# Turning the halves of a recurrent mixer kernel in another order

## The chip, the cores and the metric

The kernel runs on one core of a Trainium2 chip. The metric is the device time of one execution in microseconds (us), and a version's time is the median over its runs. A core has five engines that work side by side, each on its own queue of instructions: TensorE (PE) multiplies matrices, VectorE (DVE), ScalarE (ACT) and GpSimd (POOL) work element by element, and SyncE (SP) mostly issues DMAs. An engine takes its instructions strictly in order, and they wait for each other through semaphores, so an instruction that waits holds up all that is queued behind it.

## What is computed

The input is 4 sequences of 512 tokens with 1024 channels. Cut to what matters, the reference is

```python
xn = layernorm(x)
proj = xn @ in_proj_w.T                    # gate, hbc, dt
xBC = silu(causal_conv4(hbc))              # x, B, C per group
dt = softplus(dt + dt_bias);  dA = exp(-exp(A_log) * dt)
state_t = state_{t-1} * dA_t + (dt_t * x_t) B_t;  y_t = state_t C_t + D * x_t
s = (rms_of_group(y) * norm_weight * silu(gate)) @ out_proj_w.T
l = (xn / rms(xn)) @ [W_res, W_pre, W_post].T + base
g = silu(mix(sinkhorn(l_res), softmax(l_pre), softmax(l_post), xn))
out = x + s * g
```

The recurrence is worked out in its closed form over a sequence of 512: a matrix of decays between all pairs of tokens, multiplied by the products of C and B, is applied to dt * x. All is float32. TensorE multiplies a float32 matrix as three products of high and low parts (hi\*hi, hi\*lo, lo\*hi), so each operand that is streamed or held has to be split into both parts first.

## The kernel before

**Halves, groups, slots.** The 2048 tokens are worked in two halves of 1024 (two sequences, 8 token tiles of 128). For each half the kernel runs a front, then 8 groups of 8 heads. A group has 20 slots (SLOTS); in each, TensorE projects one tile of 128 channels for one sequence (`project`, L1101 to L1103, 24 matmuls) into one of two PSUM banks that alternate. Slots 0 to 11 carry channels that are convolved: ScalarE applies the last tap (`tap`, L616), VectorE the three others (`conv`, L839), ScalarE takes a tanh (L624), VectorE ends the silu (L851). Slots 12 to 19 are gate channels. ScalarE and VectorE also split the next weight tile into high (`split_hi`, L600) and low parts (`split_lo`, L821).

**Units.** A group's heads and sequences make 8 units, 0 to 7. For each one SP loads rows of cumulated decays (L363), ScalarE turns them into decays in two pieces (`exps`, L648 to L658, one for each of two heads), VectorE weighs them with C\*B (`weigh`, L877), TensorE transposes x (L1125), VectorE multiplies it by dt (L886), TensorE forms the products (`mult`, L1139), VectorE adds D\*x (`finish_y`, L899), ScalarE squares y (L671), and GpSimd adds up the squares (L476) and multiplies y with the gate (L467). Behind the last units come the channel sums on TensorE (L1149), a variance (L812), a root (L482), a trip through DRAM that spreads the root over the partitions (L372, L375), the scaling on GpSimd (L491) and the store (L378).

**Plans.** Which slot does which step of a unit is written out by hand in a `Plan`: FIRST for the first group of a half, LAST for the last, LATER for the others. `exp` lists the slot of each of the 16 pieces of decays, unit by unit. Slots from 20 on belong to the next group, and behind a half's last group they are worked by `drain`, which runs single slots of the old plan inside the next front, or behind the groups after the second half.

**The turn of the halves.** `front(1)` on each engine works the 8 token tiles of the second half, one t after the other, and drains slot 20 + t of the old group between. For a tile, VectorE takes statistics (`stats_of`, L933, L935), GpSimd makes the reciprocal root and the shift (`ln_rstd`, four instructions, L522 to L528), ScalarE scales the tile (`normalise`, L687), TensorE turns it in two half tiles n = 2t and 2t + 1 (`turn_stream`, L1171), ScalarE copies each half out of PSUM as the high part (`high`, L697), and VectorE takes the low part (`low`, L923). Tiles 0 to 3 have statistics and scale from before the turn, and half tiles 0 and 1 are turned in the last slot. There are three PSUM banks for the half tiles at this turn, so n = 3 waits for the low part of half tile 0. The lists STATS_AT, RSTD_AT and SCALE_AT say in which pass t of the front each tile is taken; their second entries are those of this turn.

Between them lie the small products (L1189 to L1191, 88 channels: dt and the logits), for two token tiles at a time, behind n = 5, n = 9 and at the end. They need the small weights in high (`small_hi`, ScalarE, L771) and low parts (`small_low`, GpSimd, L534). The pieces of the projection of slots 0 and 1 fill the rest of TensorE's front. Then it turns the small results back to tokens (L1219).

**Behind the front.** In slot 1 of the first group VectorE adds dt_bias to dt (z, L989), scales the logits (L993 to L997) and subtracts their maximum (L1004), all in `early`, ahead of that slot's convolution. At the top of slot 2 ScalarE takes the exponential of the logits (L706), works the softplus of z (L708 to L712, with a table load), and then splits the next weights and taps. TensorE's projection of slot 4 waits for the convolution of slot 2.

**Behind the second half** the product with out_proj_w runs in four passes, its operands loaded (L1337, L1338) and split (L1346, L1347, L1355, L1356) per 128 rows. The first pieces of it are woven into the last drained slots.

## Time and profile before

| what | value |
|---|---|
| median of 3 runs | 3055.89 us (3054.63 to 3057.09) |
| the profiled execution's own time | 3054.47 us |
| its span | 3053.0 us |
| busy time of TensorE | 3000.2 us |
| busy time of VectorE, ScalarE, GpSimd | 2128.1, 1763.6, 687.7 us |
| mean granted clock of TensorE | 0.997 |
| the front of half 0 | 0 to 45 us |
| the turn of the halves | 1160 to 1208 us |
| the last drained slots of half 1 | 2320 to 2340 us |

The span is what the trace covers; the execution's own time has 1.5 us more around it. Busy times of the engines overlap. A row of a time line has the start, the busy time, the engine, the line of the kernel, the operation, what it writes and reads, and how many such instructions the row merges; the bracket has the idle time of the engine ahead of it and who ended it. The granted clock is a share of full speed. Matmuls are pipelined, so their rows overlap a little.

### The profile page before, as it was taken

What the parts mean: (1) busy time and instruction counts of PE and PEld (TensorE: products, weight loads), DVE (VectorE), ACT (ScalarE), POOL (GpSimd) and SP (SyncE); (2) the same over time, 40 slices, a digit from 0 to 9 for tenths busy, and PEclk for the clock granted to TensorE, in tenths of its full rate; (3) what the DMA queues carried; (4) which work ended last, traced back from release to release, by engine and by line L of the source; (5) the groups of instructions that cost most, each with busy time, mean ns of one, the idle gap of its engine ahead of it and who ended that gap; (6) DMA issues with size and microseconds to landing.
All of it is one profiled execution on the core that took longest, in us unless ns stands there. A gap on an engine that the chain in (4) does not pass through costs nothing.

```text
span 3053.0 us, 45217 instructions
## 1 busy us (share of the span) xinstructions
PE 3000.2 (98%) x14352; PEld 2341.8 (77%) x14352; DVE 2128.1 (70%) x2648; ACT 1763.6 (58%) x3728; POOL 687.7 (23%) x575
## 2 busy tenths in 40 slices
PE   8999999999999998999999999999999999999998
PEld 7777777777777777777777777777777788887787
DVE  7667667576666685767666666766667878677877
ACT  5667575757666575576665757575665332234443
POOL 4222213121222134413222231212124000001112
PEclk9999999999999999999999999999999999999999
DMA  3534343443434353435243433434254444456665
GB/s 138 169 126 158 108 159 107 141 138 110 155 110 155 114 197 98 157 121 172 95 168 104 157 123 135 139 109 160 90 171 153 148 138 150 146 196 211 209 212 182
DMA packets 125532, 444.90 MB, mean 146 GB/s; under 512 B 17488, under 2 KB 21712, under 8 KB 109008
## 3 DMA queue, kind: packets, MB, share of 16 engines
q1 hardware_dynamic: 117552, 423.14, 41.1%
q0 software_dynamic: 4096, 14.68, 1.2%
q10 hardware_dynamic: 3744, 5.51, 0.6%
q8 instruction: 52, 0.85, 0.1%
q14 instruction: 88, 0.72, 0.1%
HBM read 397.86 MB, written 45.42 MB: 145 GB/s over the span
## 4 chain that ended last, share of the span: by engine, by line
PE 82%; issue 5%; DVE 4%; POOL 2%; ACT 2%; DMA 2%; DVEq 0%; SPq 0%; ACTq 0%; POOLq 0%
PE bank L1101 18%; PE bank L1103 17%; PE bank L1102 17%; PE bank L1139 9%; PE bank L1361 5%; PE bank L1362 5%; PE bank L1363 5%; PE bank L1113 2%; PE bank L1125 2%; DMA acc<-in_w_out 1%; PE bank L1149 1%; POOL gate L467 1%; DVE acc L839 1%; DVE x_lo L1356 1%; DVE x_lo L1355 1%
## 5 line engine op out<-in xcount | busy, mean ns | idle before, releaser
L1101 PE MATMUL bank<-x_hi,w_hi 128*128 128x512 f32 x2576 | 1024.6, 398 | 2.4 <-DVE acc L839 2.4
L1103 PE MATMUL bank<-x_hi,w_lo 128*128 128x512 f32 x2576 | 1003.0, 389 | 0.0
L1102 PE MATMUL bank<-x_lo,w_hi 128*128 128x512 f32 x2576 | 1000.9, 389 | 0.0
L839 DVE SCALAR_TENSOR_TENSOR acc<-bank,conv_w,acc 128x511 f32<-128x511 f32 (+2 forms) x576 | 430.8, 748 | 270.5 <-ACT acc L616 241.9
L1101 PEld LDWEIGHTS bank<-x_hi,w_hi 128*128 128x128 f32 x2576 | 484.1, 188 | 114.7 <-issue 22.2
L1103 PEld LDWEIGHTS bank<-x_hi,w_lo 128*128 128x128 f32 x2576 | 484.0, 188 | 102.6
L1102 PEld LDWEIGHTS bank<-x_lo,w_hi 128*128 128x128 f32 x2576 | 484.9, 188 | 93.6
L616 ACT ACTIVATE acc<-bank,tap_par 128x512 f32<-128x512 f32 x192 | 149.5, 779 | 517.0 <-PE bank L1103 486.0
L1361 PE MATMUL bank<-x_hi 128*128 128x512 f32 x1008 | 394.7, 392 | 8.9 <-DVE x_lo L1356 5.3
L1362 PE MATMUL bank<-x_lo,x_hi 128*128 128x512 f32 x1008 | 393.1, 390 | 0.0
L1363 PE MATMUL bank<-x_hi,x_lo 128*128 128x512 f32 x1008 | 392.9, 390 | 0.0
L877 DVE TENSOR_TENSOR units<-units,bc 128x2560 f32<-128x2560 f32 x128 | 370.4, 2893 | 5.2 <-ACT units L658 5.2
L1346 ACT ACTIVATE x_hi<-w_raw 128x1024 fp32r<-128x1024 f32 x126 | 133.6, 1060 | 390.4 <-PE bank L1363 279.8
L476 POOL TENSOR_TENSOR sums<-sums,sq 128x512 f32<-128x512 f32 x96 | 126.8, 1321 | 1010.2 <-ACT sq L671 1010.2
L652 ACT ACTIVATE units<-units,dec 128x384 f32<-128x384 f32 (+2 forms) x768 | 332.5, 499 | 0.0
L648 ACT ACTIVATE units<-units,cum 128x128 f32<-128x128 f32 x1024 | 325.0, 393 | 5.5 <-DMA units<-cum_scratch 5.5
L821 DVE TENSOR_TENSOR w_lo<-w_raw,w_hi 128x1024 fp32r<-128x1024 f32 x160 | 204.7, 1279 | 173.3 <-ACT w_hi L600 173.3
L858 DVE SCALAR_TENSOR_TENSOR gate<-th,gate 128x512 f32<-128x512 f32 x128 | 128.0, 1000 | 269.0 <-ACT gate L636 269.0
L1139 PE MATMUL bank<-units,dtx 128*64 128x512 f32 (+3 forms) x2048 | 304.9, 440 | 0.8 <-DVE units L877 0.8
L467 POOL TENSOR_TENSOR gate<-gate,units 128x512 f32<-128x512 f32 x128 | 190.8, 1495 | 345.8 <-DVE gate L858 275.8
L1139 PEld LDWEIGHTS bank<-units,dtx 128*64 128x64 f32 x2048 | 135.6, 137 | 165.4 <-issue 145.4
L1355 DVE TENSOR_TENSOR x_lo<-w_raw,x_hi 128x1024 fp32r<-128x1024 f32 x126 | 168.1, 1334 | 134.2 <-ACT x_hi L1347 133.7
(165 smaller groups left out, 3408.0 us busy)
## 6 DMA issues: line engine op xcount, KB each, us to landing
units<-cum_scratch SPq DMA_DIRECT2D x128, 1280.0 KB, 6.7
w_raw<-in_w_in SPq DMA_DIRECT2D x160, 512.0 KB, 3.7
w_raw<-y_scratch SPq DMA_DIRECT2D x128, 512.0 KB, 3.6
y_scratch<-gate SPq DMA_DIRECT2D x32, 1024.0 KB, 6.5
acc<-in_w_out SPq DMA_DIRECT2D x128, 256.0 KB, 3.8
xbc<-in_x SPq DMA_DIRECT2D x16, 512.0 KB, 5.6
units<-in_x SPq DMA_DIRECT2D x16, 512.0 KB, 3.7
rstd_b<-rc_scratch SPq DMA_DIRECT2D x32, 256.0 KB, 4.3
```

Of the source, the lines that this page charges most:

```text
L467: pool.tensor_tensor(part, part, y[:, u % 2, :], ALU.mult).then_inc(gated, 1)
L648: op = act.activation(part, part, ACT.Relu, bias=mix.cum[:, CHUNKS * q + k, head], scale=-1.0)
L652: act.activation(part, part, ACT.Exp, bias=mix.dec[:, CHUNKS * q + k, head])
L839: dve.scalar_tensor_tensor(acc[:, s % 2, back:], bank_proj[s % 2][:, 0:SEQ - back], mix.conv_w[:, at, m, 3 - back:4 - back], acc[:, s % 2, ...
L877: dve.tensor_tensor(attn[u % RING][:, :, :], attn[u % RING][:, :, :], bc[:, q, :].unsqueeze(1).to_broadcast([P, 2, SPAN]), ALU.mult).then_ ...
L1101: pe.matmul(out, w_hi[m % 2][:, k, :], hi, start=(k == 0), stop=False)
L1102: pe.matmul(out, w_hi[m % 2][:, k, :], lo, start=False, stop=False)
L1103: mm = pe.matmul(out, w_lo[m % 2][:, k, :], hi, start=False, stop=(k == KT - 1))
L1139: mm = pe.matmul(bank_y[u % 2][h * HD:(h + 1) * HD, k * P:SEQ], dtx[:, u % 2, k, h * HD:(h + 1) * HD], attn[u % RING][:, h, OFFSET[k]:OFFS ...
L1361: pe.matmul(self.bank[t][:, :], self.y_hi[n][j][:, toks], self.w_hi[n][j], start=first, stop=False)
L1362: pe.matmul(self.bank[t][:, :], self.y_hi[n][j][:, toks], self.w_lo[n][j], start=False, stop=False)
L1363: return pe.matmul(self.bank[t][:, :], self.y_lo[n][j][:, toks], self.w_hi[n][j], start=False, stop=last)
```

## The change

Six edits. (1) In the plan LAST the decays of units 5 and 7 take a slot together each (15 and 18) and those of unit 6 slots 16 and 17; the last piece was in slot 19 before. (2) At the turn VectorE takes the statistics of tile 4 in pass 1 instead of pass 0. (3) GpSimd takes the roots of tiles 5 and 6 both in pass 2, ahead of the drained slot 22 (whose last step is a multiply with the gate), and that of tile 7 in pass 5; the low part of the small weights moves from pass 1 to pass 2, behind these roots. (4) ScalarE makes the high part of the small weights in pass 1 instead of pass 0. (5) TensorE does the drained slot 21, the products of unit 7, ahead of transpose n = 3 instead of behind it. (6) VectorE's logits in slot 1 of both halves' first group come behind that slot's convolution; z stays ahead of it.

```diff
 LAST = Plan(cb=[5, 7], load=[4, 5, 7, 10, 12, 14, 15, 17], mult=[9, 11, 13, 14, 16, 18, 20, 21],
-            gate_from=CONV_SLOTS, exp=[6, 7, 8, 9, 10, 11, 11, 12, 13, 14, 15, 16, 17, 18, 18, 19])
+            gate_from=CONV_SLOTS, exp=[6, 7, 8, 9, 10, 11, 11, 12, 13, 14, 15, 15, 16, 17, 18, 18])
...
-STATS_AT = [{t: [0, 1, 2] if t == 0 else [t + 2] for t in range(NT - 2)}, {0: [4], 2: [5], 3: [6], 5: [7]}]
+STATS_AT = [{t: [0, 1, 2] if t == 0 else [t + 2] for t in range(NT - 2)}, {1: [4], 2: [5], 3: [6], 5: [7]}]
...
-RSTD_AT = [{t: [t] for t in range(NT)}, {1: [4], 3: [5], 4: [6], 6: [7]}]
+RSTD_AT = [{t: [t] for t in range(NT)}, {1: [4], 2: [5, 6], 5: [7]}]
...
                 for i in RSTD_AT[half].get(t, []):
                     ln_rstd(half, i)
-                if t == (1 if half else 2):
+                if t == 2:
                     small_low(half)
...
             for t in range(NT):
-                if t == 0 and half:
+                if t == 1 and half:
                     act.wait_ge(proj_done, SLOTS * half * GROUPS)
                     act.wait_ge(e.small_loaded, 16)
                     act.activation(small_hi, small_raw, ACT.Copy).then_inc(e.small_step, 1)
...
-        def early(half, s):
+        def early(half, s, late=False):
...
-            if s == 1:
+            if s == 1 and not late:
...
                     dve.tensor_tensor(z[:, tiles, :], part[:, :, 0:HEADS], over_tiles(dt_bias, HEADS),
                                       ALU.add).then_inc(e.dt_step, 1)
+            if s == 1 and late:
+                for i, b in enumerate(bank_small):
+                    part = b[:, 0:4 * SMALL].rearrange("p (t c) -> p t c", c=SMALL)
+                    tiles = slice(4 * i, 4 * i + 4)
                     if i == 0:
+                        dve.wait_ge(e.to_tokens, 2)
                         dve.wait_ge(e.rms_step, 4)
                     dve.tensor_tensor(logits[:, tiles, :], part[:, :, HEADS:],
...
                     if s or plan is not FIRST:
                         conv(g, at, s)
+                    if plan is FIRST and s == 1:
+                        early(half, s, late=True)
                     if s:
                         silu(g, s - 1)
...
                 if half and n == 2:
                     drain(piece, half - 1, SLOTS, SLOTS + 1)
                     pe.wait_ge(dtx_done, UNITS * g)
+                if half and n == 3:
+                    drain(piece, half - 1, SLOTS + 1, SLOTS + 2)
                 turn_stream(half, n)
-                if half and h:
+                if half and h and t > 1:
                     drain(piece, half - 1, SLOTS + t, SLOTS + t + 1)
```

## Rows read from the trace of the kernel before

**Rows 1.** The page's busy times of the engines over the span.

```profile
PE 3000.2 (98%) x14352; PEld 2341.8 (77%) x14352; DVE 2128.1 (70%) x2648; ACT 1763.6 (58%) x3728; POOL 687.7 (23%) x575
```

**Rows 2.** Waits of TensorE over the run: total, times, longest, in us.

```profile
PE bank L1171 <- DVE x_lo L923: 10.1, 3, 5.1
...
PE bank L1101 <- DVE acc L839: 2.4, 2, 1.4
```

**Rows 3.** Engines' busy time by stretches of the turn; PEclk behind POOL's.

```profile
core 0: us, PE busy (x) PEld busy (x) DVE busy (x) ACT busy (x) POOL busy (x), PEclk, DMA share, GB/s
1160.00:1170.00 10.00, 4.89 (x26) 2.37 (x24) 6.91 (x9) 7.57 (x16) 6.12 (x7) 0.83 0.12 22
1170.00:1180.00 10.00, 7.65 (x69) 6.92 (x65) 5.93 (x12) 2.73 (x4) 6.62 (x7) 1.00 0.24 83
1180.00:1190.00 10.00, 7.37 (x45) 6.79 (x45) 4.51 (x9) 5.02 (x7) 7.85 (x18) 0.83 0.28 55
```

**Rows 4.** TensorE's time line at the turn, where it waited.

```profile
1166.73 1.09 PE L1171 MATMUL bank<-ident,xbc 128*128 128x128 f32 x4 [5.11 <-DVE x_lo L923]
...
1174.09 0.63 PE L1171 MATMUL bank<-ident,xbc 128*128 128x128 f32 x4 [2.35 <-DVE x_lo L923]
...
1183.24 0.85 PE L1171 MATMUL bank<-ident,xbc 128*128 128x128 f32 x4 [2.63 <-DVE x_lo L923]
```

**Rows 5.** VectorE's time line at the start of the turn.

```profile
1160.74 1.28 DVE L933 BATCH_NORM_STATS2 rows<-xbc 128x6 f32<-128x512 f32 x2
...
1162.50 2.83 DVE L877 TENSOR_TENSOR units<-units,bc 128x2560 f32<-128x2560 f32 x1 [0.24 <-ACT units L658]
...
1165.90 1.28 DVE L923 TENSOR_TENSOR x_lo<-bank,x_hi 128x512 fp32r<-128x512 f32 x2
```

**Rows 6.** ScalarE's time line at the turn, its longest wait for GpSimd.

```profile
1180.65 1.24 ACT L687 ACTIVATE xbc<-xbc,ln_shift,rstd 128x1024 f32<-128x1024 f32 x1 [4.20 <-POOL ln_shift L528]
```

**Rows 7.** GpSimd's time line at the turn.

```profile
1169.17 1.69 POOL L534 TENSOR_TENSOR w_lo<-units,w_hi 128x704 fp32r<-128x704 f32 x1
...
1176.53 1.30 POOL L476 TENSOR_TENSOR sums<-sums,sq 128x512 f32<-128x512 f32 x1 [3.22 <-ACT sq L671]
...
1179.16 0.21 POOL L522 TENSOR_SCALAR lv<-mv 128x1 f32<-128x1 f32 x1
...
1180.38 0.24 POOL L528 TENSOR_SCALAR ln_shift<-ln_shift 128x1 f32<-128x1 f32 x1
```

**Rows 8.** DMA issues from 1160 to 1180 us: KB each, median us to landing.

```profile
xbc<-in_x SPq DMA_DIRECT2D x2, 512.0 KB, 3.5
```

**Rows 9.** VectorE's time line in slot 1 of half 1.

```profile
1208.26 0.42 DVE L989 TENSOR_TENSOR units<-bank,rows 128x256 f32<-128x256 f32 x1 [0.49 <-PE bank L1219]
...
1210.23 0.23 DVE L1004 TENSOR_TENSOR rstd_b<-rstd_b 128x64 f32<-128x64 f32 x1
1210.37 2.31 DVE L839 SCALAR_TENSOR_TENSOR acc<-bank,conv_w,acc 128x511 f32<-128x511 f32 x3
```

**Rows 10.** ScalarE's time line in slot 2 of half 1.

```profile
1210.49 0.26 ACT L706 ACTIVATE rstd_b<-rstd_b 128x64 f32<-128x64 f32 x1 [1.34 <-DVE rstd_b L1004]
...
1213.78 1.04 ACT L600 ACTIVATE w_hi<-w_raw 128x1024 fp32r<-128x1024 f32 x1
```

**Rows 11.** TensorE's time line at the start of slot 4, both halves.

```profile
57.83 0.47 PE L1101 MATMUL bank<-x_hi,w_hi 128*128 128x512 f32 x1 [1.41 <-DVE acc L839]
...
1220.40 0.47 PE L1101 MATMUL bank<-x_hi,w_hi 128*128 128x512 f32 x1 [1.00 <-DVE acc L839]
```

**Rows 12.** TensorE's time line behind half 1, where it waited.

```profile
2331.02 0.50 PE L1361 MATMUL bank<-x_hi,w_hi 128*128 128x512 f32 x1 [1.52 <-DVE x_lo L1356]
...
2340.39 0.61 PE L1361 MATMUL bank<-x_hi,w_hi 128*128 128x512 f32 x1 [1.20 <-DVE var_eps L812]
...
2369.09 0.50 PE L1361 MATMUL bank<-x_hi 128*128 128x512 f32 x1 [2.49 <-DVE x_lo L1356]
```

**Rows 13.** VectorE's time line behind half 1.

```profile
2324.24 2.83 DVE L877 TENSOR_TENSOR units<-units,bc 128x2560 f32<-128x2560 f32 x1 [1.69 <-ACT units L658]
...
2340.18 0.15 DVE L812 TENSOR_SCALAR var_eps<-bank 128x4 f32<-128x4 f32 x1
```

## The prediction

> **What bounds the kernel now.** I read four views: the page's busy times, the waits of TensorE, the granted clock by stretches, and then the time line of each engine around the places where TensorE waits. TensorE is busy for 98% of the span [rows 1]. So only its idle time, some 50 us in all, and the time it runs at the lower clock can be won, and any other engine matters only where TensorE waits for it. Two of the waits lie where the diff works. At the turn of the halves TensorE waits 10.1 us in three pieces for VectorE's x_lo (L923), and at the fifth projection slot of a half's first group it waits for a convolution (L839), 2.4 us over both halves [rows 2]. The three pieces at the turn are 5.11, 2.35 and 2.63 us [rows 4]. The granted clock is 0.83 over 1160 to 1170 and again over 1180 to 1190, and 1.00 between [rows 3]: part of each stretch ran at the lower of the two levels (1.2 instead of 2.4 GHz), which loses 10 x 0.17 = 1.7 us of work. So the turn holds 10.1 + 3.4 = 13.5 us that a better order could win. The pieces have different causes. In the first, TensorE needs x_lo of half tile 0 (1165.90), behind the weighting of the last unit (1162.50) and the statistics of tile 4 (1160.74) [rows 5]. The second has the late products behind the first transpose as its cause. In the third, ScalarE waits 4.20 us at 1180.65 for the shift of tile 5 [rows 6], because GpSimd takes its root (1179.16) only behind the addition of the last unit (1176.53) and its gate multiply [rows 7].
>
> **The change, part by part.**
>
> *1. The turn.* Times are those of the profiled execution. Up to 1160.75 us nothing that TensorE waits for moves: the decays are six pieces in five slots either way, ScalarE has room for them (3.1 us each). The decays of unit 7 are done by 1156.7 instead of 1162.5, so VectorE weighs it at 1160.75 to 1163.6 (2.83 us [rows 5]), finishes y of unit 6 by 1164.2, takes the statistics of tile 4 to 1165.65, and x_lo of half tile 0 to 1166.3. That is the same moment as before: the statistics have only changed places with the weighting. But TensorE now does the products of unit 7 meanwhile, 1163.7 to 1166.1 (sixteen matmuls, 2.4 us at the full clock), and has the transposes n = 3 and 4 behind it by 1167.7, where before it began n = 4 at 1171.1. y of unit 7 comes 3.7 us sooner. x_lo of half tile 2 follows the statistics of tile 5 (1.5 us) and is there at 1169.5. So n = 5 runs to 1170.3, the channel sums to 1171.1. Here 4.3 us are won.
>
> The small products are next, and they need the low part of the small weights (L534), which GpSimd before made at 1169.17, in 1.69 us, long ahead of its use [rows 7]. The change puts it behind the roots of tiles 5 and 6. GpSimd: the square of unit 6 is ready at 1168.7, addition and gate to 1171.3 (1.3 us each), two roots of four instructions, 1.46 us each by the one that begins at 1179.16, to 1174.2, then the low part to 1175.9. The statistics of tile 6 don't add to this: its load is issued when transpose n = 3 is done, 1167.1, and lands 3.5 us later [rows 8], so they are ready by 1172.1. **TensorE waits from 1171.1 to 1176.1**, a new wait of 5 us, and starts the small products 0.6 us later than before. It is as long as the 5.11 us one, so I charge one drop of the clock, 1.7 us. From there everything is ready: ScalarE has tiles 5 and 6 scaled, the wait of 2.63 us and its drop are gone. Before, 12.7 us lay between the start of the first small products and the end of the second; now 12.7 - 2.6 - 1.7 + 1.7 = 10.1. The turn ends at 1186.2 to 1186.6 instead of 1188.2: **a gain of 1.6 us**, 3.7 at best (no drop, 2 us less wait), nothing at worst (a landing of 5 us instead of 3.5, or slowed GpSimd work). The result's scaling on GpSimd ends 1.7 us earlier and is still well ahead of VectorE's z. SP's two last tile loads go out 0.8 and 4 us earlier, which nobody waits for.
>
> *2. The logits behind a convolution.* VectorE adds dt_bias at 1208.26, ends the logits at 1210.46 and then convolves, three instructions, 2.31 us from 1210.37 [rows 9]. Who waits for the logits is ScalarE: its exponential starts at 1210.49, and its queue holds the rest of softplus, with a table load, and then the high part of the next weights at 1213.78 [rows 10]. VectorE idles until it has them, and through its queue this delays the third convolution, for which TensorE waits 1.00 us at 1220.40, and 1.41 us at the same place of half 0 [rows 11]. So the chain from the logits to that wait has no slack at all. The convolution that goes ahead moves the exponential by the distance from its start to that of the next instruction, 2.23 us; all behind it follows. What moves forward, that convolution, was no one's wait: TensorE ran two slots without a gap. Cost: 2.23 us in this half. In half 0, where the rows repeat, ScalarE's tap is a little late: 2.1. **Sum 4.3 us.** The waits are then 3.2 and 3.5 us.
>
> The trace has no such wait in dense work, so the clock after it must be bounded. Waits of 1.00, 1.41, 2.35 and 2.49 us left the clock at 1.00; those of 2.63 (in sparse work) and 5.11 us did not. The bounds are nothing and 1.7 us each; the new waits lie above 2.63, so I take the drop: 3.4 us. The Trainium skill, "TensorE: Matmul & The Clock Gate", section "Why this matters for your kernels", says the same against this change: idle gaps of TensorE between bursts of matmuls are to be kept short, since its clock else goes back to half. By it the sum would have both drops; without it the sum is 3.4 us lower.
>
> *3. The end of half 1.* LAST's decays serve it too. VectorE's last weighting (2324.24) waits 1.69 us for ScalarE there, TensorE 1.52 us at 2331.02 for the split behind it, and 1.20 us at 2340.39 for a variance (written at 2340.18) [rows 12, 13]. With unit 7's decays done by 2320.1, the weighting starts 1.8 us earlier. That also lets ScalarE square unit 5 3 us earlier, so GpSimd's additions come sooner and hold up VectorE less. TensorE's products of unit 7 no longer wait 0.8 us, the split is ready 2.5 to 3 us earlier, and the last variance follows by 2.2 to 3. But a wait comes after: 2.49 us at 2369.09 [rows 12], at the end of a chain (variance, root, two small transfers, GpSimd's scaling, store, load, split) which moves only with that variance. What TensorE gains beyond it is waited out there. **Gain 2.5 us**; bounds nothing (the scaling is slowed more) and 3.4.
>
> *The sum*: 4.3 + 3.4 - 1.6 - 2.5 = +3.6 us. On the profiled 3054.47 us that is 3058.1. That execution lies 1.4 us under the median of the runs, 3055.89, so the median to expect is **3059.4 us**. A measurement of this kernel can tell about 0.2%, 6.1 us, from no change: my sum is inside.
>
> **The rivals.**
>
> *The clock keeps up* (no drop after the 3.3 us waits, none or one at the turn). For it: 2.49 us in dense work cost no clock. The sum is then 4.3 - 2.5 - 1.6 to 3.7 = +0.2 to -1.9, some 3055. Chance 0.25, no change that can be told.
>
> *Faster: the turn's reordering works as a whole.* If GpSimd had the low part of the small weights by 1171, the turn would lose its second and third pieces, half of the first and both drops: about 9 of the 13.5 us. With 2.5 at the end and 4.3 for the logits it gives 3055.9 - 7.2 = 3048.7. It decides if small_low waits for no more than one root. Against it: the loop takes both roots of its pass first, and TensorE can't pass the small products. Chance 0.07.
>
> *Slower: the delayed logits cost more than their convolution.* The place is ScalarE's queue at the fifth slot. VectorE has almost no idle time over the next 30 us, so 2.2 us that it loses need not be made up, and each later product of the stream mixer hangs on it. If 1.5 us more of waits follow in each half, the price is 4.3 + 3.4 + 3 = 10.7, and less 4.1 for turn and end it is +6.6: 3062.5. It decides from 6.1 - 3.6 = 2.5 us beyond my price. For it: VectorE's queue; against it: everything behind the third convolution shifts together with TensorE. Chance 0.15.
>
> *The change does nothing*: all of it is made up behind the turn. TensorE has no waits to make up with for a thousand us, so this could hold only for part 3. Chance 0.03 (3056).
>
> **The numbers.** The forecast has 0.50. Its own range is 3056 to 3062. The four rivals take the other 0.50. For 8 in 10 the range must take in the clock rival and half of each outer one: 3051.0 to 3063.0. Faster by over 0.2% (under 3049.8): 0.07. Slower (over 3062.0): 0.15. Within: 0.78.
>
> **What would show it.** In the changed profile: TensorE idle some 2 us, 2 us and then about 5 us before the first small product (L1189), released by GpSimd's w_lo; no wait near 1183; the small products over by 1186.5. At the fifth slot of both halves, waits for L839 of 3.2 to 3.5 us, with a clock under 1.00 just after. At the end no wait for L877, a variance about 2.5 us earlier and a wait for x_lo near 2369 that has grown. I am wrong if the first small product starts before 1174, if the two waits for L839 stay under 2 us, or if the end of half 1 moves by other than the sum of the first two parts, some +6 us, ahead of part 3.

## The result, and the profile after the change

The changed kernel takes 3062.78 us in the median of 22 runs (3059.68 to 3068.0). The kernel before, in 22 runs beside it, takes 3056.4 us (3054.1 to 3060.64). The ratio is 1.0021, with a 95% interval of 1.0014 to 1.0027: 6.4 us slower. That it is slower is clear; that it is slower by over 0.2%, the bound that was named, is not, since the interval begins at 0.14%. The forecast was +3.6 us, 3059.4 us in all, and the range went to 3063.0. So sign and main term were right, some 3 us were missed, and the range held by only 0.2 us, which is partly luck.

The profiled execution took 3061.02 us, with a span of 3059.5 us and a mean granted clock of 0.995 (3053.0 us and 0.997 before). Lines are shifted: the projection L1101 to L1103 is L1108 to L1110 now, L1139 is L1146, L1149 is L1156, L1171 is L1178, L1189 is L1196, L1219 is L1228, L1004 is L1009, and L1355, L1356, L1361 are L1364, L1365, L1370. This is the page's line of busy times, against [rows 1]:

```profile
PE 3004.6 (98%) x14352; PEld 2343.4 (77%) x14352; DVE 2125.8 (69%) x2648; ACT 1763.5 (58%) x3728; POOL 691.7 (23%) x575
```

The totals hardly move. The waits of TensorE at the turn (1155 to 1190 us) and the one for the convolution over the whole run say more; the columns are total, times and longest, in us. Against [rows 2]:

```profile
PE bank L1196 <- POOL w_lo L534: 4.2, 1, 4.2
PE bank L1146 <- DVE units L877: 3.0, 1, 3.0
PE bank L1178 <- DVE x_lo L923: 1.5, 1, 1.5
PE bank L1156 <- POOL sums L476: 0.5, 1, 0.5
...
PE bank L1108 <- DVE acc L839: 6.4, 2, 3.2
```

At the turn 10.1 us of one kind became 9.2 us of four kinds, with one new name at the top: the low part of the small weights. The wait for the convolution went from 2.4 to 6.4 us.

**Where the time went.** A kernel whose TensorE is busy for 98% is best compared by milestones on TensorE's own time line. Five of them cut the span into stretches: the small results turned back in half 0 (L1219 of before), the first transposes of the turn, the small results turned back in half 1, the first product of the output projection (L1361), and the matmul behind the last chain wait, at 2369.09 in [rows 12]. For each stretch the length is the difference of two starts.

| stretch | before | after | difference | forecast |
|---|---|---|---|---|
| start to L1219 | 44.69 | 45.13 | +0.4 | 0 |
| rest of half 0 | 1107.02 | 1111.17 | +4.2 | +3.8 |
| the turn | 55.94 | 56.54 | +0.6 | -1.6 |
| rest of half 1 | 1114.96 | 1118.83 | +3.9 | +3.9 |
| end of half 1, to the last chain wait | 46.48 | 44.94 | -1.5 | -2.5 |
| output passes | 683.9 | 682.9 | -1.0 | 0 |

The differences add up to 6.5 us, as the spans do. The first and the last row are not touched by the change: over the experiments below, which don't touch them either, the start took from 45.0 to 47.3 us and the output passes from 681.3 to 690.2 us. So 1 us there in any one profile means nothing, and the stretches between are to be read, not the spans.

**The logits.** This is TensorE's time line at the fifth slot of both halves, in the changed kernel, against [rows 11]:

```profile
60.08 0.47 PE L1108 MATMUL bank<-x_hi,w_hi 128*128 128x512 f32 x1 [3.21 <-DVE acc L839]
...
1227.81 0.47 PE L1108 MATMUL bank<-x_hi,w_hi 128*128 128x512 f32 x1 [3.24 <-DVE acc L839]
```

The stretches behind them, and those of the turn, against [rows 3]; PEclk, the granted clock, stands behind POOL's busy time:

```profile
core 0: us, PE busy (x) PEld busy (x) DVE busy (x) ACT busy (x) POOL busy (x), PEclk, DMA share, GB/s
60.00:70.00 10.00, 9.92 (x35) 7.43 (x35) 9.86 (x10) 4.02 (x7) 6.34 (x5) 0.83 0.32 106
1160.00:1170.00 10.00, 7.01 (x41) 4.36 (x41) 8.11 (x6) 5.53 (x11) 4.82 (x2) 1.00 0.38 141
1170.00:1180.00 10.00, 6.62 (x34) 4.48 (x30) 8.23 (x17) 4.92 (x7) 5.45 (x13) 0.68 0.30 105
1180.00:1190.00 10.00, 7.12 (x45) 7.10 (x46) 1.11 (x4) 2.46 (x4) 6.04 (x7) 0.64 0.01 0
...
1220.00:1230.00 10.00, 6.76 (x27) 5.25 (x26) 7.57 (x12) 5.39 (x7) 4.24 (x3) 0.91 0.00 0
1230.00:1240.00 10.00, 10.00 (x39) 7.50 (x39) 9.82 (x12) 4.09 (x8) 5.52 (x4) 0.92 0.50 163
```

The waits were forecast at 3.5 and 3.2 us and are 3.21 and 3.24. Behind each, part of the work ran at the lower of the two levels: 0.17 of 10 us at 60, and 0.09 and 0.08 of 10 us from 1220 to 1240. That is 1.7 us both times.

Half 0 has one small cost more, which was not forecast. These are TensorE's waits at the products of C and B (L1113, L1120 now) from 40 to 1140 us, before and after; half 1's are alike, 1.9 us in both:

```profile
PE bank L1113 <- DVE bc L868: 1.9, 5, 0.4
...
PE bank L1120 <- DVE bc L868: 2.7, 5, 0.7
```

They are 0.8 us longer. With 1.8 us more of wait at the fifth slot (3.21 less 1.41) and 1.7 us of clock this makes 4.3 us, where the stretch shows 4.2.

The delay's way through ScalarE's queue can be read off its time line in slot 2 of half 1, against [rows 10]:

```profile
1217.89 0.26 ACT L706 ACTIVATE rstd_b<-rstd_b 128x64 f32<-128x64 f32 x1 [3.56 <-DVE rstd_b L1009]
...
1221.18 1.05 ACT L600 ACTIVATE w_hi<-w_raw 128x1024 fp32r<-128x1024 f32 x1
```

ScalarE now idles 3.56 us (1.34 before) and then, behind softplus, makes the high part of the weights. From the milestone L1219 to that instruction were 1213.78 - 1207.65 = 6.13 us; now they are 1221.18 - 1212.84 = 8.34, so 2.21 us more, where 2.23 was the price.

**The turn.** Here the forecast failed. TensorE's time line, where it waited, against [rows 4]:

```profile
1169.19 3.61 PE L1146 MATMUL bank<-units,dtx 128*64 128x512 f32 x16 [2.99 <-DVE units L877]
1172.73 1.49 PE L1178 MATMUL bank<-ident,xbc 128*128 128x128 f32 x8
1175.73 0.63 PE L1178 MATMUL bank<-ident,xbc 128*128 128x128 f32 x4 [1.51 <-DVE x_lo L923]
1176.87 1.77 PE L1156 MATMUL bank<-mask,sums 128*128 128x1 f32 x8 [0.51 <-POOL sums L476]
1182.88 0.48 PE L1196 MATMUL bank<-x_hi,w_hi 128*88 128x256 f32 x1 [4.24 <-POOL w_lo L534]
```

The pieces are 2.99, 1.51, 0.51 and 4.24 us where about 2, 2 and 5 were forecast. The sixteen products of unit 7 took 3.61 us, where 2.4 were charged: the clock had dropped already there, one wait earlier than in the forecast. The cause of the first wait is seen on VectorE and GpSimd. VectorE's time line, against [rows 5]:

```profile
1165.33 3.81 DVE L877 TENSOR_TENSOR units<-units,bc 128x2560 f32<-128x2560 f32 x1
...
1169.72 1.27 DVE L933 BATCH_NORM_STATS2 rows<-xbc 128x6 f32<-128x512 f32 x2
```

and GpSimd's, against [rows 7]:

```profile
1165.18 1.27 POOL L476 TENSOR_TENSOR sums<-sums,sq 128x512 f32<-128x512 f32 x1 [6.34 <-ACT sq L671]
1166.41 3.86 POOL L467 TENSOR_TENSOR gate<-gate,units 128x512 f32<-128x512 f32 x1
...
1175.54 1.28 POOL L476 TENSOR_TENSOR sums<-sums,sq 128x512 f32<-128x512 f32 x1 [2.75 <-ACT sq L671]
1176.77 1.27 POOL L467 TENSOR_TENSOR gate<-gate,units 128x512 f32<-128x512 f32 x1
1178.12 0.22 POOL L522 TENSOR_SCALAR lv<-mv 128x1 f32<-128x1 f32 x1
...
1179.66 0.21 POOL L522 TENSOR_SCALAR lv<-mv 128x1 f32<-128x1 f32 x1
...
1181.07 1.67 POOL L534 TENSOR_TENSOR w_lo<-units,w_hi 128x704 fp32r<-128x704 f32 x1
```

The same weighing took 2.83 us in [rows 5] and takes 3.81 here. GpSimd's addition began 0.15 us ahead of it and has its normal 1.27 us; the gate multiply behind it shows 3.86 us for what takes 1.27 elsewhere, and ends within 1.2 us of the weighing's end. A reader can take this as turns at one resource: addition (to 1166.45), weighing (2.8 us, to 1169.14), gate multiply (1.2 us, to 1170.27). So not every microsecond of these durations is work. Experiment 9 tests this reading. Then the rest is as foreseen: two roots 1.54 us apart, and the low part behind both.

**The end of half 1.** Three rows of TensorE's time line, against [rows 12]:

```profile
2338.32 0.50 PE L1370 MATMUL bank<-x_hi,w_hi 128*128 128x512 f32 x1 [0.65 <-DVE x_lo L1365]
...
2347.69 0.75 PE L1370 MATMUL bank<-x_hi,w_hi 128*128 128x512 f32 x1 [1.21 <-DVE var_eps L812]
...
2376.61 0.50 PE L1370 MATMUL bank<-x_hi 128*128 128x512 f32 x1 [2.47 <-DVE x_lo L1365]
```

What lies ahead of this stretch is 9.06 us later than before (2331.67 against 2322.61). Less that, the three starts are 1.8, 1.8 and 1.5 us earlier than in [rows 12]. VectorE's time line, against [rows 13], shows why it is no more:

```profile
2331.53 2.81 DVE L877 TENSOR_TENSOR units<-units,bc 128x2560 f32<-128x2560 f32 x1
...
2334.92 1.66 DVE L1364 TENSOR_TENSOR w_lo<-w_raw,w_hi 128x1024 fp32r<-128x1024 f32 x1
2336.51 1.76 DVE L1365 TENSOR_TENSOR x_lo<-acc,x_hi 128x512 fp32r<-128x512 f32 x1
```

The weighing waits for nothing any more and starts 1.8 us earlier by the same count. But the splits behind it still take 1.66 and 1.76 us; where GpSimd is idle, they take 1.21 and 0.68 in this same trace (2324.68 and 2325.81). The forecast had GpSimd's additions out of VectorE's way, and they are not: the first one showed 2.62 us from 2332.88, held up behind the weighing.

### The profile page after: what moved, and what is told of

It reads as the page before. It is cut to its first block, busy times and chain, and to the rows that moved or that the text cites. A ratio compares the mean times of both kernels' runs of the same rounds, so it can differ in the third digit from the quotient of the medians.

```text
span 3059.5 us, 45219 instructions
## 1 busy us (share of the span) xinstructions
PE 3004.6 (98%) x14352; PEld 2343.4 (77%) x14352; DVE 2125.8 (69%) x2648; ACT 1763.5 (58%) x3728; POOL 691.7 (23%) x575
## 4 chain that ended last, share of the span: by engine, by line
PE 45%; issue 5%; DVE 4%; DMA 2%; ACT 2%; POOL 1%; DVEq 0%; SPq 0%; ACTq 0%; POOLq 0%
PE bank L1108 9%; PE bank L1110 9%; PE bank L1109 8%; PE bank L1146 4%; PE bank L1370 4%; PE bank L1372 4%; PE bank L1371 4%; DMA acc<-in_w_out 1%; PE bank L1120 1%; DVE x_lo L1365 1%; PE bank L1132 1%; DVE x_lo L1364 1%; DVE bc L1668 1%; DMA th<-in_x 1%; ACT x_hi L1356 1%
## 5 line engine op out<-in xcount | busy, mean ns | idle before, releaser
L1108 PE MATMUL bank<-x_hi,w_hi 128*128 128x512 f32 x2576 | 1024.6, 398 | 6.4 <-DVE acc L839 6.4
L1110 PE MATMUL bank<-x_hi,w_lo 128*128 128x512 f32 x2576 | 1003.0, 389 | 0.0
L839 DVE SCALAR_TENSOR_TENSOR acc<-bank,conv_w,acc 128x511 f32<-128x511 f32 (+2 forms) x576 | 430.9, 748 | 275.7 <-ACT acc L616 246.7
L1108 PEld LDWEIGHTS bank<-x_hi,w_hi 128*128 128x128 f32 x2576 | 484.4, 188 | 119.5 <-issue 26.3
L1110 PEld LDWEIGHTS bank<-x_hi,w_lo 128*128 128x128 f32 x2576 | 484.3, 188 | 103.3
L1370 PE MATMUL bank<-x_hi 128*128 128x512 f32 x1008 | 394.2, 391 | 8.2 <-DVE x_lo L1365 4.8
L1355 ACT ACTIVATE x_hi<-w_raw 128x1024 fp32r<-128x1024 f32 x126 | 133.5, 1060 | 390.7 <-PE bank L1372 252.3
L1146 PE MATMUL bank<-units,dtx 128*64 128x512 f32 (+3 forms) x2048 | 305.1, 440 | 3.0 <-DVE units L877 3.0
L1146 PEld LDWEIGHTS bank<-units,dtx 128*64 128x64 f32 x2048 | 135.6, 137 | 167.4 <-issue 145.5
L1364 DVE TENSOR_TENSOR x_lo<-w_raw,x_hi 128x1024 fp32r<-128x1024 f32 x126 | 168.6, 1338 | 134.1 <-ACT x_hi L1356 133.4
```

Source lines behind the costliest of these rows:

```text
L839: dve.scalar_tensor_tensor(acc[:, s % 2, back:], bank_proj[s % 2][:, 0:SEQ - back], mix.conv_w[:, at, m, 3 - back:4 - back], acc[:, s % 2, ...
L1108: pe.matmul(out, w_hi[m % 2][:, k, :], hi, start=(k == 0), stop=False)
L1110: mm = pe.matmul(out, w_lo[m % 2][:, k, :], hi, start=False, stop=(k == KT - 1))
L1146: mm = pe.matmul(bank_y[u % 2][h * HD:(h + 1) * HD, k * P:SEQ], dtx[:, u % 2, k, h * HD:(h + 1) * HD], attn[u % RING][:, h, OFFSET[k]:OFFS ...
L1370: pe.matmul(self.bank[t][:, :], self.y_hi[n][j][:, toks], self.w_hi[n][j], start=first, stop=False)
```

## The experiments

I had four theories to test, each against a rival: the loss comes from the logits, through ScalarE's queue; the turn's gain is eaten by the low part's place; the slow weighing is GpSimd's doing; and part of the loss is the clock. All kernels were measured beside the kernel before. "Turn" is the length of that stretch, as in the table above (55.94 us before). 0.2% is 6 us, so a median of about ten runs tells some 3 us, and below that the stretches of the profile decide.

**1. The logits alone.** The kernel before, and of the change only this:

```diff
-        def early(half, s):
+        def early(half, s, late=False):
...
-            if s == 1:
+            if s == 1 and not late:
...
+            if s == 1 and late:
...
                     if s or plan is not FIRST:
                         conv(g, at, s)
+                    if plan is FIRST and s == 1:
+                        early(half, s, late=True)
```

> The kernel before with the logits behind the convolution and nothing else. Theory A (the convolution that now goes ahead delays ScalarE's exponential, the next weights and TensorE's fifth slot by its own length, and the longer wait costs the clock): two waits for L839 of 3.2 us instead of 1.00 and 1.41 us, a granted clock of 0.83 in the 10 us behind each, together 4.0 + 3.4 = 7.4 us slower than before. Rival (most of the change's loss comes from the turn of the halves, and the delayed logits are made up by slack on VectorE): waits as in the kernel before and less than 3 us slower.

Measured: 3063.49 us against 3056.99, ratio 1.0021 (1.0012 to 1.0030), +6.5 us. TensorE's time line at the fifth slots:

```profile
60.30 0.47 PE L1108 MATMUL bank<-x_hi,w_hi 128*128 128x512 f32 x1 [3.20 <-DVE acc L839]
...
1225.49 0.47 PE L1108 MATMUL bank<-x_hi,w_hi 128*128 128x512 f32 x1 [3.23 <-DVE acc L839]
```

and the stretches behind them:

```profile
60.00:70.00 10.00, 9.70 (x40) 7.44 (x41) 9.86 (x11) 3.82 (x6) 6.55 (x5) 1.00 0.30 106
1220.00:1230.00 10.00, 6.76 (x23) 5.06 (x23) 9.76 (x16) 3.80 (x5) 4.23 (x3) 0.83 0.13 32
```

The loss of the whole change is in this part. The waits are the same to 0.01 us as in the changed kernel, but the clock is not: it dropped in half 1 and stayed at 1.00 in half 0. The rest of half 0 was 2.4 us longer than before and that of half 1 3.8 us. The waits account for 1.8 + 0.8 us in half 0 (the same 2.7 instead of 1.9 us for the products of C and B) and for 2.2 us in half 1, so the drop in half 1 cost some 1.6 us. A drop behind a 3.2 us wait is thus a matter of the execution, not a certainty; I had it as a choice between bounds, and both bounds occur.

**2. Everything but the logits.** The changed kernel with that part taken back.

```diff
-                    if plan is FIRST and s == 1:
-                        early(half, s, late=True)
```

> The changed kernel with the logits put back ahead of the convolution. Theory A: the loss of 4.1 us in the first half and 3.9 us behind the turn is gone, the turn costs 0.6 us and the end of the second half gives 2.5 us back, so about 2 us faster than before. Rival (the turn itself is what costs): no faster than before.

Measured: 3055.30 us, 0.9993 (0.9984 to 1.0002), -1.7 us; the interval takes in no change. The turn is 55.7 us, with waits of 2.99 for the weighing, 1.91 for x_lo, and then this one in TensorE's time line:

```profile
1178.90 0.48 PE L1189 MATMUL bank<-x_hi,w_hi 128*88 128x256 f32 x1 [4.96 <-POOL w_lo L534]
```

So turn and end together gain 0.2 + 1.5 us, not the 4.1 forecast. The rows give the 4.96 us to the low part, whose place the next but one tests. (Experiments 1 and 2 add up to +4.8 us, and the whole change is +6.4; each has 3 us of width, so this says nothing.)

**3. The decays alone.**

```diff
-            gate_from=CONV_SLOTS, exp=[6, 7, 8, 9, 10, 11, 11, 12, 13, 14, 15, 16, 17, 18, 18, 19])
+            gate_from=CONV_SLOTS, exp=[6, 7, 8, 9, 10, 11, 11, 12, 13, 14, 15, 15, 16, 17, 18, 18])
```

> The kernel before with only the new slots of the last group's decays. Theory A (unit 7's decays were late only behind the second half, since at the turn the statistics of tile 4 filled VectorE's time): the turn keeps its waits of 5.1, 2.4 and 2.6 us within 0.5 us, and the end of the second half is 2.5 us shorter, with the wait for L877 gone; 2.5 us faster in all. Rival (the earlier decays are worth more at the turn as well, as VectorE can weigh sooner): 4 us or more faster.

Measured: 3055.76 us, 0.9998 (0.9989 to 1.0007). The time can't tell it from no change; the stretches can. The end of half 1 is 44.76 us instead of 46.48, and VectorE no longer waits for the decays there: the whole gain of part 3 is this one edit, and it is 1.7 us (1.5 in the changed kernel), not 2.5. The turn gains nothing by it (waits of 5.57, 2.35 and 2.62 us against [rows 4]), since the statistics still stand ahead of the weighing. The first wait is even 0.46 us longer: with the decays done earlier ScalarE squares unit 5 earlier, and GpSimd's addition and multiply begin at 1160.94 and 1162.18, 3.0 and 4.6 us earlier against the turn's first transposes. Both are ahead of the weighing (1162.52), and it takes 3.60 us here.

**4. The low part back in its old place.** Experiment 2, and:

```diff
-                if t == 2:
+                if t == (1 if half else 2):
                     small_low(half)
```

> The changed kernel without the logits' edit, and with the low part of the small weights back in pass 1, behind the root of tile 4, as before. Theory A (this one step on GpSimd, queued behind two roots, is what takes back the turn's gain): TensorE's wait of 4.2 us for w_lo is gone, the small products start some 4.5 us earlier than in the changed kernel, and the whole is 4 to 6 us faster than all but the logits, that is 6 to 8 us faster than before. Rival (the turn is held by VectorE, whose weighing of unit 7 took 3.8 us instead of 2.8 beside GpSimd's gate multiply, and by the clock): the time freed comes back as a wait for x_lo at the next transposes, and it is less than 2 us faster than all but the logits.

Measured: 3050.80 us, 0.9976 (0.9966 to 0.9985), -6.2 us. The waits of TensorE at the turn:

```profile
PE bank L1139 <- DVE units L877: 3.0, 1, 3.0
PE bank L1171 <- DVE x_lo L923: 2.4, 2, 2.0
```

The wait for the low part is gone, and the turn is 51.2 us. One line of the change, a place in GpSimd's queue, costs 4.5 us at the turn, and 4.5 us between the medians of experiments 2 and 4. Up to 1.8 us of it can be the clock: by the granted clock from 1160 to 1190 us experiment 2 loses 5.2 us, experiment 4 3.4. With the line undone, the other edits of the turn gain 4.7 us. But the wait for the weighing is still 2.99 us.

**5. The gate multiply held back.** Experiment 4, and GpSimd's gate multiply of unit 5 waits until VectorE has weighed unit 7, so that it can't collide with it.

```diff
+            if hold:
+                pool.wait_ge(attn_done, UNITS * g + UNITS)
...
-                gate_y(g, u)
+                gate_y(g, u, hold=plan is LAST and half == 0 and u == 5)
```

> The kernel with the low part early, and GpSimd's gate multiply of unit 5 at the turn held until VectorE has weighed unit 7. Theory B (the weighing took 3.8 instead of 2.8 us because GpSimd's gate multiply ran beside it): the weighing is back at 2.8 us, the gate multiply at 1.3 instead of 3.9 us, TensorE's wait for L877 is 2.0 instead of 3.0 us; 1 us faster than with the low part early. Rival (the weighing is slow for another reason, such as x loads that land then): the weighing stays above 3.5 us and nothing is won.

Measured: 3051.56 us, 0.9982 (0.9973 to 0.9991), the turn 52.6 us. VectorE's time line:

```profile
1160.85 3.82 DVE L879 TENSOR_TENSOR units<-units,bc 128x2560 f32<-128x2560 f32 x1
```

and GpSimd's:

```profile
1160.70 1.28 POOL L478 TENSOR_TENSOR sums<-sums,sq 128x512 f32<-128x512 f32 x1 [6.33 <-ACT sq L673]
1164.83 1.28 POOL L469 TENSOR_TENSOR gate<-gate,units 128x512 f32<-128x512 f32 x1 [2.85 <-DVE units L879]
```

The turn is 1.4 us longer than in experiment 4, and that is the clock: from 1160 to 1190 us it loses 5.1 us here and 3.4 there. The products of unit 7 took 3.88 us here and 2.38 there, behind the same wait of 2.99 us; there the clock fell one wait later, behind 2.02 us at 1170.93 (0.66 over 1170 to 1180). The multiply is out of the way and has its normal 1.28 us, but the weighing is as slow as it was. My theory that the multiply slows it fell. What remains is the addition that begins 0.15 us ahead of it; experiment 9 holds that one.

**6. ScalarE's split ahead of softplus.** Experiment 1 with its delayed logits, but in slot 2 ScalarE does the next weights' high part and the tap first, and the exponential and softplus behind them:

```diff
-                if plan is FIRST:
+                if plan is FIRST and s != 2:
                     early(half, s)
...
+                    if plan is FIRST and s == 2:
+                        early(half, s)
```

> The kernel with only the logits behind the convolution, and ScalarE's queue in slot 2 turned: the high part of the next weights and the tap go ahead of the exponential and the softplus. Theory A (the delay reached TensorE through this queue alone): no wait for L839 at the fifth slot of either half though the logits still come late, and 2 to 3 us faster than the kernel before, 9 us faster than the logits alone. Rival (VectorE's own queue carries the delay as well: the logits' 1.4 us and the softmax stand ahead of the third convolution there): a wait of 1 to 2 us stays.

Measured: 3052.93 us, 0.9992 (0.9983 to 1.0001), -2.6 us, where experiment 1 was at +6.5. The waits of TensorE from 40 to 1300 us:

```profile
PE bank L1180 <- DVE x_lo L925: 7.5, 2, 5.1
PE bank L1122 <- DVE bc L870: 2.7, 5, 0.7
PE bank L1249 <- ACT units L740: 1.1, 2, 0.6
```

No wait for L839 is left, in either half, though the logits are as late as before. So the delay reaches the fifth slot through one place, the split and the tap behind softplus in ScalarE's queue; and [rows 10, 11] already held 2.4 us to be had there. It isn't all of the harm: the 2.7 us for the products of C and B stay (1.9 before, and in experiment 8, which has the logits in their old place), so 0.8 us in half 0 come another way. Which way is not shown.

**7. Statistics a tile later.** Experiment 4 with the statistics, scalings and roots of the turn spread so that x_lo of half tile 2 goes ahead of the statistics of tile 5:

```diff
-STATS_AT = [..., {1: [4], 2: [5], 3: [6], 5: [7]}]
-SCALE_AT = [..., {2: [4], 3: [5], 4: [6], 6: [7]}]
-RSTD_AT = [..., {1: [4], 2: [5, 6], 5: [7]}]
+STATS_AT = [..., {1: [4], 3: [5], 4: [6], 5: [7]}]
+SCALE_AT = [..., {2: [4], 4: [5], 5: [6], 6: [7]}]
+RSTD_AT = [..., {1: [4], 3: [5], 4: [6], 5: [7]}]
```

> The kernel with the low part early, and the statistics, roots and scales of tiles 5 and 6 one pass later, so that x_lo of half tiles 2 and 3 comes ahead of the statistics of tile 5. Theory (the remaining wait of 2.0 us for x_lo is this order of VectorE's): it falls to about 0.5 us, the turn is 1.5 us shorter, and up to 1.7 us more where the clock no longer falls; 1.5 to 3 us faster than with the low part early. Rival (what is freed comes back where ScalarE scales tile 5 ahead of a copy, as before the change): no faster.

Measured: 3050.75 us, 0.9983 (0.9974 to 0.9992), the turn 51.1 us as in experiment 4. The wait for x_lo shrank from 2.02 to 0.53 us, and this came in its place:

```profile
1174.65 1.05 PE L1149 MATMUL bank<-mask,sums 128*128 128x1 f32 x8 [1.51 <-POOL sums L476]
```

The channel sums need GpSimd's addition, which comes behind the same late products: where one wait was removed, the next shows, and none of my expectations had that. The clock doesn't hide a gain: the two profiles had it low at other moments (the products of unit 7 took 3.98 us here and 2.38 in experiment 4), but by the windows from 1160 to 1190 us both lose alike, 3.5 and 3.4 us. So one wait took the other's place, and no gain is shown. The 1.4 us against experiment 5 are its clock, which loses 5.1 us.

**8. Together.** The held multiply, the later statistics and the early split of ScalarE, with the logits in their old place.

> All that helped together: the changed kernel without the logits' edit, the low part early, the gate multiply held, the statistics of tiles 5 and 6 a pass later, and ScalarE's split and tap ahead of the exponential. If the gains add: 6 us of the low part early, 1 of the gate, 1.5 to 3 of the statistics, 2.4 of the splits: 11 to 12 us faster than the kernel before, about 3045 us. If they share one cause (the clock): 8 us.

Measured: 3045.62 us, 0.9970 (0.9959 to 0.9980), -10 us. By the stretches: half 0 -1.9, turn -6.4, half 1 -1.4, end -1.6. The waits at the turn are those of experiment 7, and the 1.6 us that the turn is shorter (49.5 against 51.1 us) are the clock's: it loses 1.7 us here and 3.5 there.

**9. The addition held instead.** Experiment 8, but the wait stands ahead of GpSimd's addition of unit 5 and not ahead of the multiply:

```diff
-        def add_square(g, u):
+        def add_square(g, u, hold=False):
...
+            if hold:
+                pool.wait_ge(attn_done, UNITS * g + UNITS)
```

> All that helped together, and now GpSimd's addition of unit 5 (not only its gate multiply) held until VectorE has weighed unit 7. Theory C (the one of the two engines that starts second waits for the whole instruction of the other; the weighing lost 1.0 us because the addition had begun 0.15 us ahead of it): the weighing is back at 2.8 us and TensorE's wait for it at 2.0 us instead of 3.0; 1 us faster than with only the gate held (3045.6 us), and up to 1.7 more if the clock then keeps up. Rival (something other than GpSimd slows this weighing): it stays at 3.8 us.

Measured: 3046.31 us, 0.9969 (0.9957 to 0.9982). VectorE's time line:

```profile
1159.14 2.82 DVE L881 TENSOR_TENSOR units<-units,bc 128x2560 f32<-128x2560 f32 x1
```

and TensorE's:

```profile
1162.01 2.37 PE L1143 MATMUL bank<-units,dtx 128*64 128x512 f32 x16 [1.99 <-DVE units L881]
...
1169.07 1.05 PE L1153 MATMUL bank<-mask,sums 128*128 128x1 f32 x8 [1.83 <-POOL sums L478]
```

The weighing is back at 2.82 us, TensorE waits 1.99 us for it (which is the "about 2" of the forecast), and the products run at the full clock in 2.37 us. That settles the cause. The time is the same as in experiment 8, though the small products start 1.7 us earlier (19.9 against 21.6 us behind the turn's first transposes). The addition that was held is late for the channel sums, 1.83 against 1.51 us, and above all the clock, which in experiment 8 was low over the products of unit 7, is low over the small products here, from 1170.3 on: one drop in each, 1.7 us, and it only changed its place.

**10. The low part behind one root.** Experiment 2, with the low part between the roots of tiles 5 and 6:

```diff
+                    if half and i == 5:
+                        small_low(half)
-                if t == 2:
+                if t == 2 and not half:
                     small_low(half)
```

> The changed kernel without the logits' edit, and with the low part of the small weights between the roots of tiles 5 and 6 instead of behind both. Theory A (each root ahead of it delays TensorE by its own length): the wait for w_lo, 5.0 us with both ahead, falls to 3.5 us, and 1.5 us are won. Rival (the wait is a matter of tile 6's load, which comes late): it falls by less than 0.7 us or by more than 2.5 us.

Measured: 3054.08 us, 0.9995 (0.9986 to 1.0004), the turn 55.6 us. The profiled execution was the slowest of the eleven, 3059.07 us. TensorE's time line:

```profile
1177.34 0.49 PE L1191 MATMUL bank<-x_hi,w_hi 128*88 128x256 f32 x1 [2.63 <-POOL w_lo L534]
```

The wait shrank from 4.96 to 2.63 us, by 2.3 us, more than the 1.5 of the theory and less than the 2.5 of its rival. The small products start 25.1 us behind the turn's first transposes, where experiment 2 has 26.3 (experiment 4: 21.3). In this profile nothing of it reaches the end of the turn (55.6 against 55.7 us), but the clock explains that: from 1160 to 1190 us it loses 6.9 us here and 5.2 in experiment 2. So a root ahead may well cost about its own length; this pair of profiles can't show it. My "faster" rival said that one root ahead would be enough for it to hold. It is not: the larger part of the delay stands ahead of both roots: GpSimd waits 2.76 us for the square of unit 6, and its addition and multiply take another 2.5 us. Only ahead of those is the low part in time.

**11. The wait filled.** The changed kernel, with twelve more matmuls ahead of the fifth slot's projection, into a bank that is free there; nobody reads their result.

```diff
+                if plan is FIRST and s == 4:
+                    for n in range(12):
+                        pe.matmul(core.bank[7][:, :], mix.x_hi[:, 0, 0:P], mix.x_hi[:, 0, 0:SEQ], start=True, stop=True)
```

> The changed kernel, whole, with twelve more matmuls (128 by 512, operands that lie ready, into a free bank, result unused) on TensorE ahead of slot 4's projection in each half's first group; they fill 2.7 of the 3.2 us that it waits for L839 there. Theory D (behind such a wait the clock falls and costs 1.7 us on top): the granted clock is 1.00 in the 10 us behind both places, the wait left is 0.5 us, and the kernel is 2 to 3.5 us faster than the changed one (3062.8 us) although it does more work. Rival (the clock has nothing to do with the difference): the same time as the changed kernel.

Measured: 3059.07 us, 1.0012 (1.0003 to 1.0021), +2.8 us against the kernel before, where the changed kernel without them is at +6.4. The stretches behind the waits:

```profile
60.00:70.00 10.00, 9.50 (x40) 6.90 (x39) 9.79 (x12) 2.63 (x4) 7.22 (x5) 1.00 0.30 105
1220.00:1230.00 10.00, 9.47 (x42) 7.56 (x41) 7.26 (x12) 5.40 (x7) 4.03 (x3) 1.00 0.00 0
```

Of the two waits 0.50 and 0.53 us are left, and the clock stays at 1.00. The projection starts no earlier, since its convolution is as late as before, and still half 0 is 1.6 us shorter than in the changed kernel and half 1 1.8 us. So each drop cost about the 1.7 us that the windows say. The Trainium skill, "TensorE: Matmul & The Clock Gate", section "Why this matters for your kernels", wants the idle gaps between bursts of matmuls kept short; this run agrees, 3.7 us faster with the gaps filled. It isn't so every time: in half 0 of experiment 1 the clock stayed at 1.00 behind 3.20 us.

**12. The turn's first wait filled.** Experiment 9, with two float32 matmuls ahead of the products of unit 7; nobody reads their result.

```diff
+                    for _ in range(2):
+                        pe.matmul(core.bank[7][:, :], core.ident[:, :], core.mask[:, :], start=True, stop=True)
```

> The kernel with the addition held, and two more matmuls (128 by 512 float32, about 1 us each, result unused) on TensorE ahead of unit 7's products at the turn, where it waits for the weighing. Theory D: the granted clock stays at 1.00 over the turn, 1.7 us faster than with the addition held if that one still lost its clock there, otherwise the same. Rival: the fillers run beyond the wait and it is up to 1 us slower.

Measured: 3045.66 us, 0.9969 (0.9958 to 0.9981), the turn 49.5 against 49.4 us. The granted clock is 0.83 over 1170 to 1180 in both. Nothing was won, nor lost. At the wait that was filled there was nothing to win, since the clock had stayed up behind it in experiment 9 (products in 2.37 us); the drop that is left comes behind the other short waits, which weren't filled. What would remove it stays open.

Experiments 8, 9 and 12 can't be told apart. Each is some 10 us (0.3%) faster than the kernel before and 17 us faster than the changed one.

**The turn with and without its clock.** Loss is 10 us times what the granted clock lacks to 1, added over the three windows from 1160 to 1190 us.

| | turn | loss | difference |
|---|---|---|---|
| experiment 4 | 51.2 | 3.4 | 47.8 |
| experiment 5 | 52.6 | 5.1 | 47.5 |
| experiment 7 | 51.1 | 3.5 | 47.6 |
| experiment 8 | 49.5 | 1.7 | 47.8 |
| experiment 9 | 49.4 | 1.7 | 47.7 |
| experiment 12 | 49.5 | 1.7 | 47.8 |

Without the clock the six are alike to 0.3 us. (The loss is an upper bound of what the clock cost, since a low clock during a wait costs nothing.) What is shown at the turn is the gain of the low part's old place with the new order (experiment 4). Holding the multiply or the addition, and the later statistics, moved waits about and shortened nothing beyond the clock, whose state in one profile each may be chance.

## Why the prediction was right or wrong

*Part 2, the logits: right, but for a small term.* "The waits are then 3.2 and 3.5 us" against 3.24 and 3.21, 2.21 us of delay at the split against 2.23, and 3.8 and 3.9 us forecast against 4.2 and 3.9 found. Experiment 1 puts the whole loss there and experiment 6 shows the way that most of it takes. The small term is the 0.8 us of waits for the products of C and B in half 0, put at nothing. "I take the drop: 3.4 us" held in the profiled execution. As a rule it is too sure: one of four such waits (two in the changed kernel, two in experiment 1) left the clock at 1.00. And the list of waits behind which the clock stayed up was not complete: in the same trace it was 0.83 over 2340 to 2350, behind waits of 1.52 and 1.20 us [rows 12].

*Part 1, the turn: the step that failed* is "so VectorE weighs it at 1160.75 to 1163.6 (2.83 us)". It starts when I said (1165.33 less the 4.59 us by which the turn began later is 1160.74), but takes 3.81 us. I had taken the duration from a row in which VectorE had begun first. The evidence lay in the trace of before, in this row of GpSimd's time line, which I did not use:

```profile
1163.55 2.90 POOL L476 TENSOR_TENSOR sums<-sums,sq 128x512 f32<-128x512 f32 x1 [9.29 <-ACT sq L671]
```

It ran beside the weighing of 1162.50 and shows 2.90 us where its like take 1.3: there GpSimd was the one that waited. The change moved the weighing 1.75 us earlier, and the addition 3.0 us (1163.55 before, 1165.18 less 4.59 = 1160.59 now), to just ahead of it, and so turned round who waits. The earlier addition is edit (1)'s doing, as experiment 3 shows. The prediction used it for the end of half 1 ("lets ScalarE square unit 5 3 us earlier") and not at the turn, where it let nothing move up to 1160.75 and read the new decays as "six pieces in five slots either way"; in the new plan they are in four. Of "the same moment as before" 1.0 us is lost, and behind a wait of 2.99 instead of 2 us the clock dropped already for the products of unit 7: 3.61 instead of 2.4 us (in experiment 9 the wait is 1.99 us, and they take 2.37). These two terms, 1.0 + 1.2 = 2.2 us, are the size of the miss. They pass on through the transposes behind the products and ScalarE's copy of them, behind which the square of unit 6 queues. That square, the addition behind it, the two roots and the low part follow as forecast, each 2.2 us late: w_lo is ready at 1182.74, against 1175.9 + 4.6 = 1180.5. From the first small product to the end of the turn the forecast gained 2.6 us, and 2.3 came.

*"Charge one drop of the clock" in the turn: wrong in number.* The windows from 1170 to 1190 are at 0.68 and 0.64, which loses 6.8 us where 1.7 were charged and the kernel before loses 3.4. Some of it costs nothing: the clock was low through the 4.24 us of the wait for w_lo, and the channel sums ahead of that wait (1.77 us at 1176.87) only shortened it. What counts is the products of unit 7, and the first twenty of the small ones at 0.21 us apiece, up to 1187.

*The cause of the new wait: right.* "The change puts it behind the roots of tiles 5 and 6", and experiment 4 gives 4.5 us back for that one line (up to 1.8 us of them the clock's).

*Part 3, the end of half 1: right in kind, too large.* "The weighting starts 1.8 us earlier" is met. The failed term is "GpSimd's additions come sooner and hold up VectorE less": the splits still take 1.66 and 1.76 us. So all that follows moves by 1.8 us and not by 2.5 to 3. The 2.49 us wait at the end of the chain did not grow (2.47): TensorE's work ahead of it and the chain moved together.

*The rivals.* "The clock keeps up" did not hold in the profiled execution, and did in half 0 of experiment 1. "Faster: the turn works as a whole" had its mechanism right in experiment 4, -6.2 us without the logits' part, but its point of decision wrong (experiment 10). "The delayed logits cost more than their convolution" gave nearly the time that was found, 3062.5, and mostly by the wrong cause: of its 1.5 us more of waits in each half, 0.8 came in half 0 and none in half 1, which came out at +3.9. A median that fits a rival is no evidence for it; the stretches are.

The sum over the parts: 3.6 forecast, 2.2 at the turn, 1.0 at the end of half 1, 0.35 in half 0, 0.4 ahead of it, and -1.0 in passes that the change doesn't touch, gives 6.5.

Two slips in the sums change nothing: 3055.89 + 3.6 is 3059.5, not 3059.4, and the turn's "3.7 at best" is the gain with no drop alone; with "2 us less wait" as well it would be over 5.

## What to carry to other kernels

Before you move a small instruction of an in-order engine behind others, count its whole queue up to the new place, and place it by the consumer that has the least slack, not by its cost. When you move an instruction of VectorE with two operands in SBUF, look at what GpSimd starts around the new moment, and at what the same change does to that: who starts first keeps its normal duration, and the other shows the wait as duration. Compare kernels that a busy TensorE bounds by milestones on its time line, and set the granted clock of each stretch beside its length before you call a difference a gain. Read a clock drop behind a wait of about 3 us as a chance, not as a yes or no.

## What the runs showed of the hardware

**A blocked instruction looks like a slow one.** At the turn the weighing took 2.82 or 2.83 us where it began ahead of GpSimd (the kernel before and experiments 1, 6, 9 and 12), and 3.80 to 3.83 us in the changed kernel and in experiments 2, 4, 5, 7, 8, 10 and 11, where GpSimd's addition had begun 0.14 or 0.15 us earlier (3.82 less 2.82 is what was left of the addition's 1.28 us, to about 0.15). It holds over the whole run: of the 128 weighings of the kernel before, the 116 that began with no GpSimd instruction under way took 2.8 us, and the 12 that began beside one took 3.1 to 3.9 us. GpSimd's multiply showed 3.86 us behind it, and 1.28 when held off. The Trainium skill, "SBUF — State Buffer", section "Who interferes with whom", says that a VectorE instruction with two inputs in SBUF contends with a GpSimd instruction that reads SBUF, since its second input comes through the read interface that the two share. That whoever issues first has the shared pair for the whole instruction while the other "**fully blocks** (not throttle)" it says of VectorE's 2-port modes. The trace agrees with the first, and shows the second for this two-input instruction as well, with these numbers. What I had not expected is how it looks: no wait is shown for the blocked instruction, only a longer duration.

**The clock after a wait of 3 us is not fixed.** Four waits of 3.20 to 3.24 us in dense work (experiment 1 and the changed kernel) gave three drops and one full clock. The wait of 2.98 to 3.00 us for the weighing stands in eight profiles: the changed kernel and experiments 2, 4, 5, 7, 8, 10 and 11. The products behind it took 3.61 to 4.07 us in seven of them and 2.38 us in experiment 4. In experiment 4 the clock then fell behind the next wait, of 2.02 us. Behind the 1.99 us of experiment 9 they took 2.37 us. Shorter waits aren't safe either: in the output passes, dense work, the clock fell to half behind a wait of 1.84 us in experiment 2 (at 2867.9 us, 0.91 and 0.92 over 2860 to 2880) and of 1.97 us in experiment 10 (at 2867.8 us). A drop cost 1.6 to 1.8 us, by the stretches of experiments 1 and 11.
